# The last merge level's N: a copy on ScalarE in place of a masked product on VectorE

## The chip, the cores and the metric

The kernel runs on one core of a Trainium2 chip. The metric is the device time of one execution in microseconds (us); lower is better.

## What is computed

The reference is one transformer layer on an input of 4 sequences x 512 positions x 256: a gated delta-rule attention with 16 key heads and 32 value heads of width 128, a residual with layer norm, a mixture of 8 experts (top 2) plus a shared expert, and a second residual with layer norm. The attention is where nearly all of the time goes:

```python
def step(state, xs):
    q_t, k_t, v_t, g_t, b_t = xs
    state = state * jnp.exp(g_t)[..., None, None]
    kv = jnp.einsum('bhk,bhkv->bhv', k_t, state)
    delta = (v_t - kv) * b_t[..., None]
    state = state + jnp.einsum('bhk,bhv->bhkv', k_t, delta)
    out = jnp.einsum('bhk,bhkv->bhv', q_t, state)
    return (state, out)
```

The kernel computes this in chunks of 128 positions, and for each chunk and value head it needs the inverse of a 128x128 unit triangular matrix M that is made of keys, decays and betas.

## The kernel before, in words

**Bodies.** There are 64 bodies (`BODIES`), one for each pair of key head and sequence. A body has 4 chunks and 2 value heads, so 8 matrices M ("cells"), each 128x128. Six stages of work of up to four different bodies are interleaved: `ORDER` holds one list for each engine, written by hand, of entries (name, index, bodies ahead), and each engine walks through its own list once in each round. An engine carries out its list strictly in order. All waits are on semaphores that count finished operations.

**The inverse.** It is found by merging diagonal blocks: `X` holds the inverse of the blocks of size s in 16 bits, `XT` its transpose, and a level i joins blocks of size s = `LEVELS[i]` (2, 4, ..., 64) in pairs. A level has these steps:

- `join` on TensorE (L1024): 8 matmuls, one for each cell, of `mhiT` with the left column blocks of `X`, into PSUM bank `IB[1 - i % 2]`.
- `join` on VectorE (L1314): the product from PSUM times the mask `lev`, into `N[:, i]`. The mask keeps the diagonal and the block below it. For the last level (i = 5, s = 64) the left half of the columns is written, and the mask there is the identity in rows 0 to 63 and all ones in rows 64 to 127.
- `growx` on TensorE (L1034), a product of `XT` and `N`, and on ScalarE (L1215) the copy of it from PSUM into `X`.
- from level 2 on `growt` on TensorE (L1040) and on ScalarE (L1218), the same for `XT`.

`fill_n` (L838) sets all six parts of `N` to the identity once, at the start; later steps write only the left column blocks.

**After the last level.** `newton` (L1051, L1052) multiplies M with `X` for a correction, in two halves of 4 cells; half 0 waits for `X` of level 5 (`s_x`), half 1 for `XT` of level 5 (`s_xt`). Then VectorE's `res` (L1318) and TensorE's `finish` (L1059), VectorE's `tt` (L1324), and the chunk by chunk solution (`solve` L1075, `write` L1085, `read` L1063, `out` L1101 and L1102).

**Around the last level.** TensorE's list has, in this order: `solve` 3, `out` 2, `join` 5, `out` 3, `growx` 5, `growt` 5, `vtp` 0 to 2 (L992, transposes of v of a later body, which wait for ScalarE's `silu` 3), `newton` 0 and 1, `vtp` 3, `gate` 0 (L1001, which waits for ScalarE's `vals`). ScalarE's list has `u` 3 (L1223), `silu` 3 (L1183), `power` 0 (L1230: four squares, each with its accumulator read; it waits for VectorE's `og` 0), `growx` 5, `growt` 5, `vals` 0 (L1205), `power` 1, `vals` 1, `zs` 0 (L1211). VectorE's list has `conv` 10 and 11 (L1278), `og` 0 (L1351), `join` 5, `og` 1, `scan` 0 (L1284), `res` 0 and 1.

`silu` 3 and `vtp` belong to the body after the one whose levels are merged, `u`, `power` and `og` to the body of the round before.

The last round runs with the mixture of experts' first work in the free places (`drain`), and after it that part runs alone.

Of the kernel before, what the change touches and what calls it, by code (L numbers as in the profile page):

```python
# [9 lines left out]
ACT = mybir.ActivationFunctionType  # L10
# [11 lines left out]
LEVELS = [2, 4, 8, 16, 32, 64]  # L22
# [20 lines left out]
        ("proj", 6, 3), ("join", 3, 2), ("write", 2, 1), ("proj", 7, 3),  # L43
    ],
    "scalar": [
        ("growx", 3, 1), ("silu", 2, 2), ("growt", 3, 1), ("growx", 4, 1), ("growt", 4, 1), ("u", 3, 0),
        ("silu", 3, 2), ("power", 0, 0), ("growx", 5, 1), ("growt", 5, 1), ("vals", 0, 2), ("power", 1, 0),
        ("vals", 1, 2), ("zs", 0, 2), ("u", 0, 1), ("turn", 0, 0), ("tap", 0, 3), ("zs", 1, 2), ("tap", 1, 3),
        ("silu", 0, 3), ("turn", 1, 0), ("growx", 0, 2), ("u", 1, 1), ("squares", 0, 3), ("kraw", 0, 3),
# [1 line left out]
        ("growt", 2, 2), ("tap", 3, 3),  # L51
    ],
    "vector": [
        ("conv", 10, 2), ("conv", 11, 2), ("og", 0, 0), ("join", 5, 1), ("og", 1, 0), ("scan", 0, 2), ("res", 0, 1),
        ("res", 1, 1), ("tt", 0, 1), ("tt", 1, 1), ("scan", 1, 2), ("m", 0, 2), ("m", 1, 2), ("p", 0, 2), ("s", 0, 1),
        ("p", 1, 2), ("x0", 0, 2), ("conv", 0, 3), ("conv", 1, 3), ("rhs", 1, 1), ("conv", 2, 3), ("join", 0, 2),
        ("conv", 3, 3), ("acc", 0, 0), ("conv", 4, 3), ("turned", 0, 2), ("join", 1, 2), ("s", 1, 1), ("conv", 5, 3),
# [19 lines left out]
def build_kernel(nc, x_rows, x_cols, w_heads, w_ab, conv_w, dt_bias, a_log, gamma, w_out,  # L77
                 rms_w, router_w, gate_up, down, tri, levels16, neg_mask, ident16, iota8, exponents, out):
    ctx = ExitStack()
    with ctx:  # L80
# [3 lines left out]
        def sem(name):  # L84
            return ctx.enter_context(nc.semaphore(name))
# [3 lines left out]
        PB, IB, OB = bank[0:2], bank[2:4], bank[6:8]  # L89
# [22 lines left out]
        conv = sb("conv", [P, GROUPS, SEQ])  # L112
# [26 lines left out]
        N = sb("N", [P, len(LEVELS), CELLS, P], F16)  # L139
        res = mloT  # L140
# [4 lines left out]
        og = sb("og", [P, CELLS, P])  # L145
# [56 lines left out]
        s_np = sem("s_np")  # L202
        s_ident = sem("s_ident")
        s_n = sem("s_n")
        s_xgp = sem("s_xgp")
        s_x = sem("s_x")
        s_xtp = sem("s_xtp")
# [54 lines left out]
        def blocks(t, i, odd):  # L262
            s = LEVELS[i]
            return t.rearrange("p x (b two s) -> p x b two s", two=2, s=s)[:, :, :, odd]

        def packed(t, i):
            return t[:, :].rearrange("p (x b s) -> p x b s", x=CELLS, s=LEVELS[i])

        MATMUL_LEVELS = len(LEVELS) - TURNED

        def bank4(t):
            return t[:, :].rearrange("p (x n) -> p x n", x=4)
# [681 lines left out]
        def _(pe):  # L954
            gates_tensor(pe)

            def run(name, i, n):
# [67 lines left out]
                                       blocks(X[:, x:x + 1, :], i, 0), start=True, stop=True)  # L1025
                    mm.then_inc(s_np, 1)
                elif name == "growx":
                    pe.wait_ge(s_n, 6 * n + i + 1)
                    if 0 < i <= TURNED:
                        pe.wait_ge(s_xv, TURNED * n + i)  # L1030
                    if i > TURNED:
# [3 lines left out]
                                       start=True, stop=True)  # L1035
                    mm.then_inc(s_xgp, 1)
                elif name == "growt":
                    pe.wait_ge(s_n, 6 * n + i + 1)
                    for x in range(CELLS):
                        mm = pe.matmul(IB[1 - i % 2][:, x * 64:(x + 1) * 64], N[:, i, x, :], blocks(XT[:, x:x + 1, :], i, 1),  # L1040
                                       start=True, stop=True)
# [1 line left out]
                elif name == "newton":  # L1043
# [3 lines left out]
                    else:  # L1047
                        pe.wait_ge(s_xt, MATMUL_LEVELS * (n + 1))
                    for x in range(4):
# [110 lines left out]
        @block.scalar  # L1160
        def _(act):
            gates_scalar(act)
            act.wait_ge(s_const, CONSTS)

            def run(name, i, n):
                p, q, head = n % 2, n % 3, n // B
                if name == "tap":
                    g = COLS_OF[i]
                    act.wait_ge(s_proj, n * 4 + i + 1)
                    act.activation(conv[:, g, :], PB[i % 2][:, :], ACT.Copy,  # L1170
                                   scale=cw_all[:, head, g * TAPS + 3:g * TAPS + 4]).then_inc(s_tap, 1)
                elif name == "silu":
                    act.wait_ge(s_conv, 12 * n + 3 * i + 3)
                    if i == 0 and n > 2:
                        act.wait_ge(s_kq, 2 * (n - 2))
                        act.wait_ge(s_ksp, 3 * (n - 2))
                    if i == 1 and n > 1:
                        act.wait_ge(s_kq, 2 * (n - 1))
                        act.wait_ge(s_qe, n - 1)
                    if i == 2 and n > 0:  # L1180
                        act.wait_ge(s_vtp, 2 * n)
                    dst = (kT[:, q], qT[:, p], vT[:, 0], vT[:, 1])[i]
                    act.activation(dst, conv[:, COLS_OF[i], :], ACT.Silu).then_inc(s_silu, 1)  # L1183
                elif name == "squares":
                    act.wait_ge(s_ktp, n * 2 + i + 1)
                    if n > 0:
                        act.wait_ge(s_sq, 8 * (n - 1) + 4 * i + 4)
                    if n > 1:
                        act.wait_ge(s_ssk, n - 1)
                        act.wait_ge(s_epsq, n - 1)  # L1190
                    for c in range(CH):
                        act.activation(sqj[:, i, c, :], PB[i][:, c * P:(c + 1) * P], ACT.Square,  # L1192
                                       accum_out=ssum[:, p, i, c:c + 1]).then_inc(s_sq, 1)
                elif name == "kraw":
                    act.wait_ge(s_ktp, n * 2 + 1)
                    if n > 0:
                        act.wait_ge(s_keys, n)
                    act.activation(kraw[:, :, :], bank4(P0), ACT.Copy).then_inc(s_kraw, 1)  # L1198
                elif name == "vals":
                    act.wait_ge(s_vtp, n * 2 + i + 1)  # L1200
                    act.wait_ge(s_nk, n + 1)
                    if n > 1:
                        act.wait_ge(s_r, 6 * (n - 1))
                    for c in range(2):
                        act.activation(vals[:, p, 4 * i + 2 * c:4 * i + 2 * c + 2, :], bank4(PB[i])[:, 2 * c:2 * c + 2], ACT.Copy,  # L1205
                                       scale=nr[:, p, 0, 2 * i + c:2 * i + c + 1]).then_inc(s_vals, 1)
                elif name == "zs":
                    act.wait_ge(s_zp, n * 2 + i + 1)
                    if n > 1:
                        act.wait_ge(s_og, 2 * (n - 1))  # L1210
                    act.activation(zs[:, p, 2 * i:2 * i + 2, :], PB[i][:, :].rearrange("p (c n) -> p c n", c=2),  # L1211
                                   ACT.Silu).then_inc(s_zs, 1)
                elif name == "growx":
                    act.wait_ge(s_xgp, 6 * n + i + 1)
                    act.activation(blocks(X[:, :, :], i, 0), packed(IB[i % 2], i), ACT.Copy).then_inc(s_x, 1)  # L1215
                elif name == "growt":
                    act.wait_ge(s_xtp, MATMUL_LEVELS * n + i - TURNED + 1)
                    act.activation(blocks(XT[:, :, :], i, 1), packed(IB[1 - i % 2], i), ACT.Copy).then_inc(s_xt, 1)  # L1218
                elif name == "u":
                    act.wait_ge(s_up, n * 4 + i + 1)  # L1220
                    if n > 0:
                        act.wait_ge(s_pup, 2 * n)
                    act.activation(U[:, 2 * i:2 * i + 2, :], R1[:, 0:256].rearrange("p (v n) -> p v n", v=VH),  # L1223
                                   ACT.Copy, scale=1.0 if i else -1.0).then_inc(s_u, 1)
                elif name == "power":
                    act.wait_ge(s_og, n * 2 + i + 1)
                    if n > 0:
                        act.wait_ge(s_mse, n)
                    for x in range(4 * i, 4 * i + 4):
                        act.activation(og2[:, x, :], og[:, x, :], ACT.Square, scale=P ** -0.5,  # L1230
                                       accum_out=ms[:, 0, x:x + 1]).then_inc(s_ms, 1)
                elif name == "turn":
                    act.wait_ge(s_gtp, n * 2 + i + 1)
                    if n > 0:
                        act.wait_ge(s_opp, 2 * (n - 1) + i + 1)
                    act.activation(half(ogT, i), bank4(OB[i]), ACT.Copy).then_inc(s_gt, 1)  # L1236

            def drain(name, i, n):
                if (name, i, n) == ("growt", 3, BODIES - 1):
                    prepare_scalar(act, 3, 0)  # L1240
                elif (name, i, n) == ("power", 1, BODIES - 2):
                    prepare_scalar(act, 7, 0)
                elif (name, i, n) == ("u", 1, BODIES - 1):
                    gate_scalar(act, 0)
                elif (name, i, n) == ("u", 2, BODIES - 1):
                    gate_scalar(act, 1)
                    gate_scalar(act, 2)
                elif (name, i, n) == ("power", 1, BODIES - 1):
                    gate_scalar(act, 3)
                elif (name, i, n) == ("turn", 0, BODIES - 1):  # L1250
                    gate_scalar(act, 4)

            for name, i, n in rounds(ORDER["scalar"]):
                run(name, i, n)
                if n == 0 and (name, i) == ("tap", 0):
                    decays_scalar(act)
                if n == 0 and (name, i) == ("silu", 0):
                    rows_scalar(act)
                drain(name, i, n)
            moe_scalar(act)  # L1260
# [193 lines left out]
```

## Time and profile before

| | |
|---|---|
| median of 3 runs | 2317.08 us (2313.6 to 2317.55) |
| profiled execution, span from first to last instruction | 2315.6 us |
| profiled execution, own time outside the span | not listed; the median of the runs lies 1.5 us above the span |
| instructions | 53,894 |
| TensorE busy | 98% of the span |
| VectorE busy | 84% |
| ScalarE busy | 57% |
| GpSimd busy | 52% |
| round to round | 31.98 us |

Busy shares are means over the whole span. Within a round each engine's list has dense and thin stretches, so what the table says of ScalarE (57%) need not hold where the change is made. TensorE's matmuls are recorded from issue to end and overlap their neighbours; the times at which they start say more than their busy time.

### The profile page before, as it was taken

What the parts mean: (1) busy time and instruction counts of PE and PEld (TensorE: products, weight loads), DVE (VectorE), ACT (ScalarE), POOL (GpSimd) and SP (SyncE); (2) the same over time, 40 slices, a digit from 0 to 9 for tenths busy, and PEclk for the clock granted to TensorE, in tenths of its full rate; (3) what the DMA queues carried; (4) which work ended last, traced back from release to release, by engine and by line L of the source; (5) the groups of instructions that cost most, each with busy time, mean ns of one, the idle gap of its engine ahead of it and who ended that gap; (6) DMA issues with size and microseconds to landing.
All of it is one profiled execution on the core that took longest, in us unless ns stands there. A gap on an engine that the chain in (4) does not pass through costs nothing.

```text
span 2315.6 us, 53894 instructions
## 1 busy us (share of the span) xinstructions
PE 2275.0 (98%) x20046; PEld 1784.7 (77%) x20046; DVE 1953.3 (84%) x3427; ACT 1326.1 (57%) x4125; POOL 1204.2 (52%) x1199
## 2 busy tenths in 40 slices
PE   6899999999999999999999999999999999999998
PEld 3687888878888778888788887888877888776665
DVE  5788888888888888888888888888888888885665
ACT  4565666656666656666566665666666666653110
POOL 4456555555555556555655556565565655552100
PEclk8999999999999999999999999999999999999999
DMA  4011111111001110111110111101111010120000
GB/s 140 20 38 56 38 38 38 56 38 56 27 30 56 38 56 32 44 38 56 38 48 28 38 56 38 56 20 56 38 56 38 30 46 38 38 90 1 28 10 19
DMA packets 32115, 98.46 MB, mean 43 GB/s; under 512 B 4336, under 2 KB 9840, under 8 KB 31600
## 3 DMA queue, kind: packets, MB, share of 16 engines
q1 hardware_dynamic: 31856, 95.02, 11.8%
q8 instruction: 161, 2.64, 0.5%
q14 instruction: 98, 0.80, 0.1%
HBM read 92.39 MB, written 2.62 MB: 41 GB/s over the span
## 4 chain that ended last, share of the span: by engine, by line
PE 97%; DVE 2%; ACT 1%; issue 1%; DMA 0%; POOL 0%; POOLq 0%; DVEq 0%; SPq 0%; ACTq 0%
PE bank L974 19%; PE bank L1001 10%; PE bank L1120 10%; PE bank L1075 5%; PE bank L548 5%; PE bank L1102 5%; PE bank L1014 5%; PE bank L1101 4%; PE bank L1034 4%; PE bank L1085 4%; PE bank L1024 4%; PE bank L1063 4%; PE bank L984 3%; PE bank L992 3%; PE bank L1040 3%; PE bank L1110 3%
## 5 line engine op out<-in xcount | busy, mean ns | idle before, releaser
L1278 DVE SCALAR_TENSOR_TENSOR conv<-bank,cw_all,conv 128x511 f32<-128x511 f32 (+2 forms) x768 | 564.7, 742 | 45.2 <-ACT conv L1170 40.3
L974 PE MATMUL bank<-xT,w_kh 128*128 128x512 f32 x1024 | 531.0, 602 | 2.8 <-ACT kraw L1198 1.8
L1170 ACT ACTIVATE conv<-bank,cw_all 128x512 f32<-128x512 f32 x256 | 176.8, 691 | 245.4 <-PE bank L974 245.4
L1314 DVE TENSOR_TENSOR N<-bank,lev 128x512 f16<-128x512 f32 x384 | 258.9, 674 | 56.7 <-PE bank L1024 56.7
L1215 ACT ACTIVATE X<-bank 128x512 f16<-128x512 f32 x384 | 229.0, 596 | 100.6 <-PE bank L1034 100.6
L1120 PE MATMUL bank<-wo,ogT 128*128 128x256 f32 x1024 | 268.7, 385 | 0.0
L887 POOL TENSOR_TENSOR keys<-kraw,kfac 128x1024 f32<-128x1024 f32 x64 | 121.4, 1897 | 277.8 <-PE bank L1085 277.5
L1001 PE MATMUL bank<-w_kh,xT 128*128 128x256 f32 x1024 | 263.9, 391 | 0.1
L926 POOL TENSOR_TENSOR ms<-ms,epsq 128x8 f32<-128x8 f32 x64 | 12.8, 199 | 388.7 <-ACT og L1230 388.7
L1024 PEld LDWEIGHTS bank<-X,mhiT 128*128 128x128 f16 x3072 | 135.9, 98 | 101.0 <-issue 46.5
L1034 PEld LDWEIGHTS bank<-N,XT 128*128 128x128 f16 x3072 | 131.8, 98 | 106.3 <-DVE N L1314 52.8
L1223 ACT ACTIVATE U<-bank 128x256 f32<-128x256 f32 x256 | 100.9, 394 | 183.0 <-PE bank L1075 183.0
L1001 PEld LDWEIGHTS bank<-w_kh,xT 128*128 128x128 f32 x1024 | 180.7, 191 | 25.9 <-issue 1.0
L1120 PEld LDWEIGHTS bank<-wo,ogT 128*128 128x128 f32 x1024 | 180.2, 191 | 18.3 <-issue 1.0
L1102 PE MATMUL bank<-U,pT 128*128 128x128 f32 x1024 | 192.6, 280 | 0.0
L974 PEld LDWEIGHTS bank<-xT,w_kh 128*128 128x128 f32 x1024 | 161.2, 192 | 11.6 <-issue 3.3
L1192 ACT ACTIVATE sqj<-bank 128x128 f16<-128x128 f32 x512 | 134.4, 280 | 61.3 <-PE bank L984 61.2
L1308 DVE STREAM_TRANSPOSE XT<-X 128x1024 f16<-128x1024 f16 x128 | 158.7, 1240 | 9.0 <-ACT X L1215 0.7
L1034 PE MATMUL bank<-N,XT 128*128 128x64 f16 x3072 | 154.4, 193 | 9.5 <-DVE N L1314 9.5
L935 POOL TENSOR_TENSOR og<-og,ms 128x512 f32<-128x512 f32 x128 | 159.2, 1244 | 5.0
L1236 ACT ACTIVATE ogT<-bank 128x512 f32<-128x512 f32 x128 | 76.0, 593 | 149.6 <-PE bank L1110 149.6
L1101 PE MATMUL bank<-S,qE 128*128 128x128 f32 x768 | 158.7, 288 | 0.1
(181 smaller groups left out, 5651.2 us busy)
## 6 DMA issues: line engine op xcount, KB each, us to landing
egb<-rows SPq DMA_DIRECT2D x64, 512.0 KB, 4.9
ecb<-rows SPq DMA_DIRECT2D x64, 512.0 KB, 4.0
w_kh<-w_heads SPq DMA_DIRECT2D x16, 768.0 KB, 6.0
wo_raw<-w_out SPq DMA_DIRECT2D x16, 256.0 KB, 6.2
xT<-x_cols SPq DMA_DIRECT2D x4, 512.0 KB, 5.9
xT<-gate_up SPq DMA_DIRECT2D x1, 2048.0 KB, 7.7
ecb<-x_rows SPq DMA_DIRECT2D x3, 512.0 KB, 3.7
out<-og SPq DMA_DIRECT2D x3, 512.0 KB, 2.9
```

Source lines behind the costliest of these rows:

```text
L935: pool.tensor_tensor(half(og, i), half(og, i), ms[:, 2, 4 * i:4 * i + 4].unsqueeze(2).broadcast_to([P, 4, P]), ALU.mult).then_inc(s_on, 1)
L974: mm = pe.matmul(PB[j % 2][:, :], w[:, k, g * P:(g + 1) * P], xT[:, k, b * SEQ:(b + 1) * SEQ], start=(k == 0), stop=(k == KT - 1))
L1001: mm = pe.matmul(PB[h][:, 256 * c:256 * c + 256], xT[:, k, t * P:(t + 1) * P], w[:, k, 512:768], start=(k == 0), stop=(k == KT - 1))
L1024: mm = pe.matmul(IB[1 - i % 2][:, x * 64:(x + 1) * 64], mhiT[:, x, :], blocks(X[:, x:x + 1, :], i, 0), start=True, stop=True)
L1034: mm = pe.matmul(IB[i % 2][:, x * 64:(x + 1) * 64], XT[:, x, :], blocks(N[:, i, x:x + 1, :], i, 0), start=True, stop=True)
L1101: pe.matmul(dst, qE[:, p, x, :], S[:, c, v * P:(v + 1) * P], start=True, stop=False)
L1102: mm = pe.matmul(dst, pT[:, p, x, :], U[:, x, :], start=(c == 0), stop=True)
L1120: mm = pe.matmul(OB[h][:, 256 * c:256 * c + 256], ogT[:, 2 * i + v, :], wo[:, head % 2, v, :], start=(v == 0), stop=(v == VH - 1))
L1170: act.activation(conv[:, g, :], PB[i % 2][:, :], ACT.Copy, scale=cw_all[:, head, g * TAPS + 3:g * TAPS + 4]).then_inc(s_tap, 1)
L1215: act.activation(blocks(X[:, :, :], i, 0), packed(IB[i % 2], i), ACT.Copy).then_inc(s_x, 1)
L1278: dve.scalar_tensor_tensor(conv[:, g, m:], PB[j % 2][:, 0:SEQ - m], cw_all[:, head, g * TAPS + 3 - m:g * TAPS + 4 - m], conv[:, g, m:], op ...
L1314: dve.tensor_tensor(blocks(N[:, i], i, 0), packed(IB[1 - i % 2], i), blocks(lev[:, 1 + i:2 + i, :], i, 0).broadcast_to(shape), ALU.mult).t ...
```

## The change

At level 5 VectorE's multiplication by the mask is gone from its list. ScalarE gets a new entry `last`, between `u` 3 and `silu` 3, that copies partitions 64 to 127 of the product from PSUM to `N[:, 5]`. Partitions 0 to 63 are no longer written; they keep the identity of `fill_n`. TensorE's `growx` and `growt` of level 5 wait for the new semaphore `s_nlast`; those of the other levels wait for `s_n`, which now counts 5 for each body.

```diff
     "scalar": [
-        ("growx", 3, 1), ("silu", 2, 2), ("growt", 3, 1), ("growx", 4, 1), ("growt", 4, 1), ("u", 3, 0),
+        ("growx", 3, 1), ("silu", 2, 2), ("growt", 3, 1), ("growx", 4, 1), ("growt", 4, 1), ("u", 3, 0), ("last", 0, 1),
         ("silu", 3, 2), ("power", 0, 0), ("growx", 5, 1), ("growt", 5, 1), ("vals", 0, 2), ("power", 1, 0),
     "vector": [
-        ("conv", 10, 2), ("conv", 11, 2), ("og", 0, 0), ("join", 5, 1), ("og", 1, 0), ("scan", 0, 2), ("res", 0, 1),
+        ("conv", 10, 2), ("conv", 11, 2), ("og", 0, 0), ("og", 1, 0), ("scan", 0, 2), ("res", 0, 1),
@@ tensor, growx and growt
-                    pe.wait_ge(s_n, 6 * n + i + 1)
+                    if i < LAST_LEVEL:
+                        pe.wait_ge(s_n, LAST_LEVEL * n + i + 1)
+                    else:
+                        pe.wait_ge(s_nlast, n + 1)
@@ scalar
+                elif name == "last":
+                    act.wait_ge(s_np, 6 * n + 6)
+                    if n == 0:
+                        act.wait_ge(s_ident, len(LEVELS))
+                    act.activation(blocks(N[:, LAST_LEVEL], LAST_LEVEL, 0)[64:], packed(IB[0], LAST_LEVEL)[64:],
+                                   ACT.Copy).then_inc(s_nlast, 1)
```

## Rows read from the trace of the kernel before

**Rows 1.** The page: part 1 (TensorE), part 4 (the chain that ended last).

```profile
PE 2275.0 (98%) x20046; PEld 1784.7 (77%) x20046; DVE 1953.3 (84%) x3427; ACT 1326.1 (57%) x4125; POOL 1204.2 (52%) x1199
...
PE 97%; DVE 2%; ACT 1%; issue 1%; DMA 0%; POOL 0%; POOLq 0%; DVEq 0%; SPq 0%; ACTq 0%
```

**Rows 2.** Windows: stretch, its length, then busy time of each engine, PEclk.

```profile
1156.00:1163.00 7.00, 7.00 (x102) 6.53 (x99) 6.75 (x12) 6.27 (x19) 2.92 (x3) 1.00 0.01 4
```

**Rows 3.** Timeline of TensorE from join 5 on: start, length, instruction.

```profile
1160.03 0.40 PE L1024 MATMUL bank<-X,mhiT 128*128 128x64 f16 x8
1160.27 0.47 PE L1101 MATMUL bank<-S,qE 128*128 128x128 f32 x2
...
1160.79 0.39 PE L1101 MATMUL bank<-S,qE 128*128 128x128 f32 x2
1161.02 0.39 PE L1102 MATMUL bank<-U,pT 128*128 128x128 f32 x2
1161.29 0.41 PE L1034 MATMUL bank<-N,XT 128*128 128x64 f16 x8
...
1161.76 0.85 PE L992 MATMUL bank<-tri_sb,vT 128*128 128x128 f32 x6
1162.48 0.23 PE L1051 MATMUL bank<-X,mhiT 128*128 128x128 f16 x1
```

**Rows 4.** Timeline of VectorE, same stretch.

```profile
1160.55 0.68 DVE L1314 TENSOR_TENSOR N<-bank,lev 128x512 f16<-128x512 f32 x1
1161.44 0.69 DVE L1351 TENSOR_TENSOR og<-bank,zs 128x512 f32<-128x512 f32 x1 [0.21 <-PE bank L1102]
```

**Rows 5.** Timeline of ScalarE, same stretch.

```profile
1158.58 0.60 ACT L1215 ACTIVATE X<-bank 128x512 f16<-128x512 f32 x1 [0.61 <-PE bank L1034]
1159.07 0.59 ACT L1218 ACTIVATE XT<-bank 128x512 f16<-128x512 f32 x1
1159.55 0.39 ACT L1223 ACTIVATE U<-bank 128x256 f32<-128x256 f32 x1
1160.07 0.63 ACT L1183 ACTIVATE vT<-conv 128x512 f32<-128x512 f32 x1
1160.66 0.31 ACT L1230 ACTIVATE og<-og 128x128 f32<-128x128 f32 x1
...
1161.85 0.57 ACT L1215 ACTIVATE X<-bank 128x512 f16<-128x512 f32 x1
```

**Rows 6.** The same copy of level 5 in the first and last full round.

```profile
106.62 0.57 ACT L1215 ACTIVATE X<-bank 128x512 f16<-128x512 f32 x1
...
2057.21 0.57 ACT L1215 ACTIVATE X<-bank 128x512 f16<-128x512 f32 x1
```

**Rows 7.** Groups by line: ScalarE's copy of 64 partitions at the start.

```profile
L357 ACT ACTIVATE zs<-bank 64x512 f32<-64x512 f32 x2 | 1.2, 591 | 10.8 <-PE bank L389 10.8
```

**Rows 8.** ScalarE's timeline: a silu and the copy behind it.

```profile
1176.61 0.62 ACT L1183 ACTIVATE kT<-conv 128x512 f32<-128x512 f32 x1
1177.13 0.59 ACT L1236 ACTIVATE ogT<-bank 128x512 f32<-128x512 f32 x1
```

**Rows 9.** Timeline of VectorE: level 5 of body 0.

```profile
72.78 0.69 DVE L1314 TENSOR_TENSOR N<-bank,lev 128x512 f16<-128x512 f32 x1 [0.36 <-PE bank L1024]
```

**Rows 10.** Timelines of ScalarE and TensorE: level 5 of the last body.

```profile
2088.12 0.60 ACT L1215 ACTIVATE X<-bank 128x512 f16<-128x512 f32 x1 [0.32 <-PE bank L1034]
...
2086.24 0.40 PE L1024 MATMUL bank<-X,mhiT 128*128 128x64 f16 x8
```

**Rows 11.** Windows early and late (as rows 2), and TensorE's timeline at 2078.

```profile
82.00:90.00 8.00, 7.29 (x41) 4.66 (x39) 6.89 (x13) 2.32 (x5) 6.63 (x7) 1.00 0.01 2
...
2078.00:2080.00 2.00, 1.78 (x25) 1.73 (x26) 1.27 (x4) 0.61 (x2) 0.00 (x0) 0.66 0.48 172
2080.00:2082.00 2.00, 1.95 (x23) 1.73 (x21) 1.01 (x3) 0.86 (x2) 0.00 (x0) 0.50 0.03 11
...
2078.22 0.41 PE L1034 MATMUL bank<-N,XT 128*128 128x64 f16 x8 [3.28 <-DVE N L1314]
```

More of the change, by code:

```diff
@@ L204, in build_kernel @@
         s_n = sem("s_n")
+        s_nlast = sem("s_nlast")
         s_xgp = sem("s_xgp")
@@ L269, in build_kernel @@
         MATMUL_LEVELS = len(LEVELS) - TURNED
+        LAST_LEVEL = len(LEVELS) - 1
         def bank4(t):
@@ L1037, in run @@
                 elif name == "growt":
-                    pe.wait_ge(s_n, 6 * n + i + 1)
+                    if i < LAST_LEVEL:
+                        pe.wait_ge(s_n, LAST_LEVEL * n + i + 1)
+                    else:
+                        pe.wait_ge(s_nlast, n + 1)
                     for x in range(CELLS):
```

## The prediction

> **What bounds the kernel now.** I read the page first, then the chain of waits, then the timelines of three engines over the same seven microseconds of one round. The page says that TensorE is busy 98% of the span and that 97% of the chain that ended last is TensorE's [rows 1]. So what counts is whether TensorE is made to wait, and a microsecond taken off VectorE or ScalarE is worth nothing by itself. The shares of VectorE (84%) and ScalarE (57%) suggest that ScalarE has room and VectorE has not. That is the mean. In the stretch where the change is made ScalarE is busy 6.27 us of 7 and VectorE 6.75 of 7 [rows 2]: both are full there. The reader should therefore look at what each of them holds up at that place.
>
> VectorE first. TensorE's join 5 begins at 1160.03 and ends at 1160.43. VectorE's masked product begins at 1160.55, when og 0 makes room, and ends at 1161.23 [rows 3, 4]. In the meantime TensorE does out 3, and growx 5 begins at 1161.29. The last two pairs of out 3 begin at 1160.79 and 1161.02, 0.23 us apart [rows 3], so TensorE would have been ready at about 1161.24: the masked product costs TensorE 0.05 us in a round. After it VectorE idles 0.21 us until TensorE has ended out 3, and only then begins og 1 at 1161.44 [rows 4]. So VectorE's next work is released by TensorE, not by the end of the product, and taking the product away starts nothing sooner.
>
> ScalarE next. u 3 begins at 1159.55, silu 3 at 1160.07, power 0 at 1160.66, growx 5's copy at 1161.85 [rows 5], and with 6.27 us of work in 7 there is hardly a gap between them. Growx 5's matmuls end at 1161.29 + 0.41 = 1161.70 [rows 3], so the copy of X at 1161.85 waits for its place behind power 0, not for TensorE. It ends at 1161.85 + 0.57 = 1162.42 and newton 0 begins on TensorE at 1162.48 [rows 3, 5]. The six vtp matmuls before it began at 1161.76 and end at 1162.61 by the record, 0.85 us [rows 3]; but a matmul's record runs on while the next is issued (join 5's 0.40 beside the 0.24 after which its successor starts), and with some 0.16 us less for that TensorE is free at about 1162.45. The copy of X arrives just in time, with no slack at all. This is the place that decides: any delay of ScalarE's run from silu 3 to growx 5 goes into TensorE one for one.
>
> **The change part by part.** Removed: 64 masked products of 0.67 us on VectorE. By the above they are worth 0.05 us each on TensorE at growx 5, and VectorE's 0.6 us lies in front of a wait for TensorE, worth nothing.
>
> Added: one ScalarE copy of 64 partitions x 512 elements. The trace has this shape: the two copies of 64x512 from PSUM at the start take 591 ns, and the copies of 128x512 take 570 to 600 [rows 5, 7]. Half the partitions do not halve the time, and I take 0.59. What follows a copy starts 0.48 or 0.49 us after it (1158.58, 1159.07, 1159.55) [rows 5], because neighbours overlap; what follows a silu starts 0.52 after it (1176.61, 1177.13) [rows 8].
>
> Moved: everything on ScalarE behind it. The new copy waits for join 5, which ends at 1160.43, and ScalarE starts some 0.04 us after such an end, so it begins at 1160.47. Queued behind it are silu 3 (vtp 0 waits for it), power 0 (GpSimd's power and scaling of og wait for 0 and 1 together), growx 5 (newton 0), growt 5 (newton 1) and vals 0 (gate 0). Step by step:
>
> - silu 3: 1160.47 + 0.49 = 1160.96, where it was 1160.07. It ends at 1161.59, before vtp 0 would start (1161.76), so vtp is not held up.
> - power 0: 1160.96 + 0.52 = 1161.48, where it was 1160.66.
> - copy of X: power 0's eight instructions take 1161.85 - 1160.66 = 1.19 us, so 1162.67 to 1163.25, where it was 1161.85 to 1162.42: 0.82 to 0.83 later.
> - newton 0: from 1162.48 to about 1163.31, so TensorE idles about 0.83 us in front of it.
>
> The new N ends at 1160.47 + 0.59 = 1161.06, ahead of TensorE's 1161.24, so the 0.05 us at growx 5 is saved, but what stands behind it then waits for X all the same: it is part of the idle time at newton 0 and not a gain of its own. Growt 5's copy and vals 0 keep their distance from X, so newton 1 and gate 0 move by the same 0.83 and add nothing. Res, finish and tt on VectorE, and GpSimd's work on og, move with TensorE and ScalarE.
>
> Is it given back later? ScalarE has room after vals 1, TensorE has not: it issues without such gaps for the rest of the round, and the others wait for it. Nothing on TensorE is paced by something that this shift leaves where it was. So the round grows from 31.98 to 32.81 us.
>
> How many rounds: the same copy stands at 106.62 in the first round that has all this work and at 2057.21 in the last [rows 6]; (2057.21 - 106.62) / 31.98 = 61, so 62 rounds, each with the same 0.57 us and the same neighbours. Two bodies differ. Body 0 has no power 0 and no u 3 in front. VectorE's product runs from 72.78 to 73.47 there, straight after its wait for TensorE [rows 9]; ScalarE's copy is 0.1 us shorter, and this gains 0.1 us. In the last body join 5 ends at 2086.64 and the copy of X begins at 2088.12, released by TensorE [rows 10]. Now the new copy begins at 2086.68, power 0 at 2087.17, X at 2088.36: 0.24 us lost.
>
> Sum: 62 x 0.83 = 51.5; 51.5 - 0.1 + 0.2 = 51.6 us. The span 2315.6 becomes 2367.2. The median of the runs shown lies 1.5 us above the span, which gives 2368.7.
>
> Bounds of the unknown: the copy writes to partitions 64 to 127 only, of which no row exists. If it took its place at 0.40 us (the steps between ScalarE's copies are 0.48 and 0.49) the round would lose 0.74, in all 46 us: 2363. If nothing overlapped (0.59 for the copy, 0.63 for silu) it would lose 1.03, in all 64 us: 2381.
>
> **A rule against the trace.** The masked product has 0.68 us on VectorE and a copy 0.59 on ScalarE, and VectorE has the higher share of the two (84 against 57%) [rows 1, 4, 7]. The Trainium skill, page "Perfetto Trace Analysis", section "Optimizing Scalar/DVE Operations", says that where VectorE is saturated, handing some of its work to ScalarE may make sense. By that rule the change would be a gain; what it would be worth is the first rival below. The step it leaves out is that ScalarE is itself full at this place.
>
> **The rivals.**
>
> *Not slower.* ScalarE's delay is hidden, and what is left is the earlier growx 5: 0.05 us x 64 = 3 us, so 2314. For this newton 0 must find X ready at 1162.45, that is, ScalarE's run may slip by 0.03 us and no more, or TensorE must have 0.8 us of other work ready in front of newton 0. It has only the vtp matmuls, which it has already used. For it speaks VectorE's high share; against it all of rows 3 and 5. Chance 3%, nearly all of it within 0.2%.
>
> *Part of it comes back.* The longer round lets waits elsewhere shrink, for instance where TensorE waits for VectorE's N of level 4 behind two conv steps. If half of 0.83 is recovered: 62 x 0.42 = 26 us, 2343. Against it: those waits follow from TensorE's own matmuls of the level before and shift with it. Chance 7%.
>
> *Nothing overlaps on ScalarE,* or the copy waits longer for join 5: 2375 to 2381 as above. Chance 10%.
>
> *The clock falls.* After TensorE had idled 3.28 us up to 2078.22 the granted clock was 0.66 and 0.50 in the next two windows of 2 us, which is the lower of its levels (1.2 instead of 2.4 GHz) [rows 11]. Such a fall costs 2 x 0.34 + 2 x 0.50 = 1.7 us. If it came in each round: 62 x 1.7 = 105 us more, 2474. Against it: from 82 to 90 TensorE was busy 7.29 of 8 us and kept the clock at 1.00 [rows 11], and one idle time of 0.8 us in 32.8 is less. Chance 4%. The Trainium skill, "Perfetto Trace Analysis", section "Matmul Optimizations", says that TensorE scales its power with its use, so matmuls should come back to back; by that rule too an added idle time can cost more than itself, and the two windows agree with it for a long one.
>
> **How the numbers follow.** The forecast (2361 to 2375) has 76%, the four rivals 3, 7, 10 and 4%. The range must leave out no more than 2 in 10: from 2358 to 2380 it holds the forecast and nearly all of the case without overlap. A measurement of this kernel can tell about 0.2% (4.6 us) from no change. Slower by more than that has 96%, no change 3%, faster 1%.
>
> **What would show it.** In the changed profile: TensorE's waits get a line "matmul of newton (or its weight load) waits for ScalarE's X", some 0.8 us, in 62 rounds; the round is 32.8 us; silu 3 begins half a microsecond after the new copy; TensorE's busy share falls by some 2 points; and growx 5 follows out 3 without a gap. I am wrong if newton 0 still follows vtp 2 directly, if the round has shrunk somewhere else, or if windows in mid-run have a granted clock below 1.00.

## The result and the profile after

The changed kernel takes 2384.29 us (median of 4 runs, 2382.66 to 2385.7), the kernel before on the same chip 2317.32 us: a ratio of 1.0294 (95% interval 1.028 to 1.0309), 67.0 us slower. The forecast was 51.6 us slower, 2368.7, with a range up to 2380: the direction and the place were right, the size was short by 15 us, and the time lies outside the range.

These are the lines of the changed kernel's page that answer to [rows 1]:

```profile
PE 2286.1 (96%) x20046; PEld 1789.8 (75%) x20046; DVE 1921.7 (81%) x3363; ACT 1366.7 (57%) x4189; POOL 1203.8 (50%) x1199
...
PE 87%; ACT 7%; issue 4%; DVE 1%; POOL 1%; DMA 0%; POOLq 0%; DVEq 0%; SPq 0%
```

TensorE's share of the chain that ended last falls from 97 to 87%, and ScalarE has 7% of it where it had 1. TensorE's work is the same (20046 matmuls), VectorE has 64 instructions fewer and ScalarE 64 more. ScalarE's share of busy time is 57% as before; nothing on this line shows that it is now in the way.

The round's length comes from the copy of `kraw`, which stands once in a round. The lines are the row of this tile in a long stretch (count, shortest/median/longest ns, first and last start), first of the kernel before, then of the changed one:

```profile
L1198 ACT ACTIVATE kraw<-bank x40: 614/624/626, 604.2 to 1851.3; 128x512 f32<-128x512 f32 x40
```

```profile
L1206 ACT ACTIVATE kraw<-bank x39: 622/624/626, 621.5 to 1877.8; 128x512 f32<-128x512 f32 x39
```

(1851.3 - 604.2) / 39 = 31.98 us before, (1877.8 - 621.5) / 38 = 33.06 us after. The round has grown by 1.08 us, and 62 rounds of it are 67.0 us, the whole difference. The forecast had 32.81.

Now TensorE's timeline of one round of the changed kernel, from join 5 on (L1026), with out 3, growx 5 (L1039), growt 5 (L1048), vtp (L994) and newton 0 (L1059); it answers to [rows 3]:

```profile
1195.71 0.40 PE L1026 MATMUL bank<-X,mhiT 128*128 128x64 f16 x8
...
1196.69 0.39 PE L1110 MATMUL bank<-U,pT 128*128 128x128 f32 x2
1196.91 0.40 PE L1039 MATMUL bank<-N,XT 128*128 128x64 f16 x8
...
1197.44 0.87 PE L994 MATMUL bank<-tri_sb,vT 128*128 128x128 f32 x6
1199.23 0.23 PE L1059 MATMUL bank<-X,mhiT 128*128 128x128 f16 x1 [0.92 <-ACT X L1229]
```

Growx 5 begins 0.22 us after the last pair of out 3, where it was 0.27: the 0.05 us are there. Newton 0 begins 3.52 us after join 5 began, where it was 2.45, and the row names what it waited for: ScalarE's copy of X. In the kernel before, the table of waits of the whole run has this wait once, 0.6 us. In the changed kernel it has it 63 times (total us, times, longest us):

```profile
PEld bank L1059 <- ACT X L1229: 72.9, 63, 1.3
PE bank L1059 <- ACT X L1229: 58.1, 63, 1.2
```

And ScalarE's timeline of the same round, which answers to [rows 5]:

```profile
1195.22 0.39 ACT L1237 ACTIVATE U<-bank 128x256 f32<-128x256 f32 x1
1196.14 0.59 ACT L1225 ACTIVATE N<-bank 64x512 f16<-64x512 f32 x1 [0.53 <-PE bank L1026]
1196.76 0.63 ACT L1191 ACTIVATE vT<-conv 128x512 f32<-128x512 f32 x1
1197.29 0.29 ACT L1244 ACTIVATE og<-og 128x128 f32<-128x128 f32 x1
...
1198.37 0.19 ACT L1244 ACTIVATION_READ_ACCUMULATOR og<-og 128x1 f32 x1
1198.58 0.60 ACT L1229 ACTIVATE X<-bank 128x512 f16<-128x512 f32 x1
```

The reader should look at the steps from start to start. The new copy begins 0.43 us after join 5 (forecast 0.44) and lasts 0.59 (forecast 0.59). Silu 3 begins 0.62 after it, not 0.49: the copy ends at 1196.73 and silu starts only then. Silu to the first square is 0.53 (forecast 0.52). The copy of X begins 0.21 after the start of the last accumulator read, when that has ended (1198.56), where in the kernel before all such steps are about 0.09; and it lasts 0.60, where it was 0.57. So two steps have lost their overlap, 0.13 and 0.12 us, and the copy of X is 0.03 longer. In the other direction goes the first square, which took a step of 0.22 us before and takes 0.20 now. The sum, 0.26 us, is the difference between 0.83 and 1.08, to within the rounding of the rows. Why these two, when the other steps of ScalarE's list are as long as before, is what the experiments had to find out. An instruction that starts only when the one before it has ended is called held from here on.

### The profile page after: what moved, and what is told of

Its sections match the earlier page's. It is cut to its first block, busy times and chain, and to the rows that moved or that the text cites. A ratio compares the mean times of both kernels' runs of the same rounds, so it can differ in the third digit from the quotient of the medians.

```text
span 2384.0 us, 53894 instructions
## 1 busy us (share of the span) xinstructions
PE 2286.1 (96%) x20046; PEld 1789.8 (75%) x20046; DVE 1921.7 (81%) x3363; ACT 1366.7 (57%) x4189; POOL 1203.8 (50%) x1199
## 4 chain that ended last, share of the span: by engine, by line
PE 87%; ACT 7%; issue 4%; DVE 1%; POOL 1%; DMA 0%; POOLq 0%; DVEq 0%; SPq 0%
PE bank L976 18%; PE bank L1003 10%; PE bank L1128 9%; PE bank L1083 5%; PE bank L1016 5%; PE bank L550 5%; PE bank L1026 4%; PE bank L1093 4%; PE bank L1110 4%; PE bank L1071 3%; PE bank L1039 3%; ACT og L1244 3%; PE bank L1109 3%; PE bank L986 2%; PE bank L1118 2%
## 5 line engine op out<-in xcount | busy, mean ns | idle before, releaser
L1328 DVE TENSOR_TENSOR N<-bank,lev 128x512 f16<-128x512 f32 x320 | 215.4, 673 | 55.8 <-PE bank L1026 55.8
L1039 PEld LDWEIGHTS bank<-N,XT 128*128 128x128 f16 x3072 | 137.1, 98 | 102.7 <-DVE N L1328 51.9
L1026 PEld LDWEIGHTS bank<-X,mhiT 128*128 128x128 f16 x3072 | 135.8, 98 | 100.9 <-issue 46.5
L1039 PE MATMUL bank<-N,XT 128*128 128x64 f16 x3072 | 153.9, 193 | 9.4 <-DVE N L1328 8.7
```

The source lines that it names most:

```text
L1026: mm = pe.matmul(IB[1 - i % 2][:, x * 64:(x + 1) * 64], mhiT[:, x, :], blocks(X[:, x:x + 1, :], i, 0), start=True, stop=True)
L1039: mm = pe.matmul(IB[i % 2][:, x * 64:(x + 1) * 64], XT[:, x, :], blocks(N[:, i, x:x + 1, :], i, 0), start=True, stop=True)
L1328: dve.tensor_tensor(blocks(N[:, i], i, 0), packed(IB[1 - i % 2], i), blocks(lev[:, 1 + i:2 + i, :], i, 0).broadcast_to(shape), ALU.mult).t ...
```

## The experiments

### A copy over all 128 partitions

```diff
-                    act.activation(blocks(N[:, LAST_LEVEL], LAST_LEVEL, 0)[64:], packed(IB[0], LAST_LEVEL)[64:],
+                    act.activation(blocks(N[:, LAST_LEVEL], LAST_LEVEL, 0), packed(IB[0], LAST_LEVEL),
                                    ACT.Copy).then_inc(s_nlast, 1)
```

> The new ScalarE copy covers all 128 partitions instead of 64 to 127, everything else as in the changed kernel (rows 0 to 63 of N then hold the product itself instead of the identity). Theory A, that ScalarE does not overlap an instruction with the one before it where the starting partition differs from that of the last write to, or the last read from, the same memory: both steps close, silu 3 starts 0.49 us after the copy instead of 0.62 and the copy of X 0.09 after the last accumulator read instead of 0.21; the round loses 0.24 us, 62 rounds 15 us: 2369 us, where the forecast was. Theory B, that any copy put in this place waits like this (it follows a wait for TensorE, or ScalarE's queue runs dry): 2384 us, steps unchanged.

Measured: 2365.12 us against 2314.19 of the kernel before on that chip, a ratio of 1.0215 (1.0198 to 1.0232); the round is 32.78 us, from the row of `kraw`:

```profile
L1206 ACT ACTIVATE kraw<-bank x39: 621/623/625, 617.0 to 1862.6; 128x512 f32<-128x512 f32 x39
```

```profile
1186.84 0.60 ACT L1225 ACTIVATE N<-bank 128x512 f16<-128x512 f32 x1 [0.52 <-PE bank L1026]
1187.33 0.62 ACT L1191 ACTIVATE vT<-conv 128x512 f32<-128x512 f32 x1
...
1188.92 0.19 ACT L1244 ACTIVATION_READ_ACCUMULATOR og<-og 128x1 f32 x1
1189.02 0.58 ACT L1229 ACTIVATE X<-bank 128x512 f16<-128x512 f32 x1
```

Both steps close: 0.49 and 0.10. With twice the partitions the copy lasts 0.60 us where it lasted 0.59, and the round is 0.28 us shorter. This kernel leaves the mask out (rows 0 to 63 of `N` hold the product where the identity belongs), so it measures the hold and is no replacement for the changed kernel. Theory B falls. The forecast's own arithmetic (32.81, and 51 us slower) describes this kernel, not the one that was asked for: the difference here is 50.9 us.

### 64 partitions, but the lower ones

```diff
-... LAST_LEVEL, 0)[64:], packed(IB[0], LAST_LEVEL)[64:],
+... LAST_LEVEL, 0)[:64], packed(IB[0], LAST_LEVEL)[:64],
```

> The copy covers partitions 0 to 63 in place of 64 to 127 (so rows 64 to 127 of N are never updated: this part of the merge is left out). Theory A, the starting partition counts: steps 0.49 and 0.09, about 2369 us, as with 128 partitions. Rival, the number of partitions counts (64 against 128 in the neighbours): steps 0.62 and 0.21, 2384 us.

Measured: 2366.76 us in one run, a round of 32.76 us, steps of 0.49 to 0.50 and 0.09 to 0.10. This kernel leaves out the rows of `N` that the merge needs. The number of partitions plays no part; where they start does.

### Reads and writes apart

```diff
-... LAST_LEVEL, 0)[64:], packed(IB[0], LAST_LEVEL)[64:],
+... LAST_LEVEL, 0)[64:], packed(IB[0], LAST_LEVEL)[:64],
```

> The copy reads partitions 0 to 63 of the bank and writes partitions 64 to 127 of N (N then holds other rows: the last merge is wrong in value). Theory A with reads and writes apart: the write sets the memory of silu 3's hold, so silu 3 still starts 0.62 us after the copy; the read from PSUM started at partition 0, so the copy of X starts 0.09 us after the accumulator read. 0.12 x 62 = 7 us less than the changed kernel, 2377 us. Rival, one cause for both steps: both stay (2384) or both go (2369).

```diff
-... LAST_LEVEL, 0)[64:], packed(IB[0], LAST_LEVEL)[64:],
+... LAST_LEVEL, 0)[:64], packed(IB[0], LAST_LEVEL)[64:],
```

> The mirror image: the copy reads partitions 64 to 127 of the bank and writes partitions 0 to 63 of N (N holds other rows: the last merge is wrong in value). Theory A: silu 3 starts 0.49 us after the copy (its write starts where the last one did, and it reads SBUF), while the copy of X, the next to read PSUM, still starts 0.21 us after the accumulator read. About 2377 us. Rival, one cause for both steps: 2384 or 2369.

Measured: 2372.52 and 2378.62 us, one run each, where about 2377 was expected of both, and rounds of 32.91 and 32.93 us. Both kernels put other rows into `N` than the merge needs. The rounds differ by 0.02 us and the single times by 6. Most of the 6 us lies before the rounds: in the first 80 us TensorE's mean granted clock was 0.94 in the first of the two and 0.85 in the second, and the same copy of `kraw` stands at 614.9 and at 619.7 us. So the rounds and the steps are the better evidence. ScalarE's timeline where the copy reads partition 0 on and writes partition 64 on:

```profile
1187.05 0.59 ACT L1225 ACTIVATE N<-bank 64x512 f16<-64x512 f32 x1 [0.53 <-PE bank L1026]
1187.66 0.63 ACT L1191 ACTIVATE vT<-conv 128x512 f32<-128x512 f32 x1
...
1189.28 0.18 ACT L1244 ACTIVATION_READ_ACCUMULATOR og<-og 128x1 f32 x1
1189.37 0.57 ACT L1229 ACTIVATE X<-bank 128x512 f16<-128x512 f32 x1
```

And where it reads partition 64 on and writes partition 0 on:

```profile
1192.10 0.59 ACT L1225 ACTIVATE N<-bank 64x512 f16<-64x512 f32 x1 [0.53 <-PE bank L1026]
1192.60 0.62 ACT L1191 ACTIVATE vT<-conv 128x512 f32<-128x512 f32 x1
...
1194.19 0.19 ACT L1244 ACTIVATION_READ_ACCUMULATOR og<-og 128x1 f32 x1
1194.40 0.60 ACT L1229 ACTIVATE X<-bank 128x512 f16<-128x512 f32 x1
```

Reads and writes hold different instructions. A write that starts at partition 64 holds the next instruction that writes SBUF from partition 0 (silu 3: 0.61 against 0.50). A read of PSUM that starts at 64 holds the next instruction that reads PSUM from partition 0, and that is the copy of X, with nine instructions in between (0.21 against 0.09); silu and the squares in between read SBUF and are not held. The two prices, 0.13 and 0.15 us a round against 32.78, add up to the 0.28 of the changed kernel.

The Trainium skill states this for VectorE, on the page "VectorE: DVE Perf Modes", section "Two Vector instructions with no wait between them": an instruction is held until all earlier ones have finished where its input or output starts in another quarter of the partitions than the last read from, or the last write to, the same memory. The section speaks of Vector instructions only. On ScalarE the changed kernel and these four variants of its copy agree with it, with 0.12 to 0.13 us for each hold. They tried starts at 0 and 64 alone, and of the two orders only the instruction at 0 behind one at 64: the new copy itself waits for TensorE, so a hold in front of it would not show.

### The copy twice

A second copy of the same 64 partitions into a scratch area (the squares' unread output `sqj`), directly in front of the first (the semaphore `s_extra` and the squares' wait for it are not shown):

```diff
+                    act.wait_ge(s_sq, 8 * min(n + 1, BODIES - 1) + 8)
+                    act.activation(sqj[64:, 0].rearrange("p c (y s) -> p (c y) s", s=64),
+                                   packed(IB[0], LAST_LEVEL)[64:, :, 0], ACT.Copy).then_inc(s_extra, 1)
                     act.activation(blocks(N[:, LAST_LEVEL], LAST_LEVEL, 0)[64:], packed(IB[0], LAST_LEVEL)[64:],
```

> A second, useless copy of the same 64 partitions of the bank (into a scratch area) directly in front of the new one on ScalarE. Theory, ScalarE's delay reaches TensorE one for one through the copy of X: the second copy adds one step of 0.49 us (same starting partitions, so it overlaps) to each of 62 rounds, 30 us: 2415 us. Rival, the delay is partly absorbed further on or newton is held by something else: clearly less than 30 us. Rival, it also makes growx 5 late (N would end 0.3 us after TensorE is ready): no more than the same 30 us, since newton waits behind it anyway.

Measured: 2415.89 us in one run, the round 33.55 us, 0.49 longer than the changed kernel's. ScalarE's timeline:

```profile
1211.59 0.59 ACT L1229 ACTIVATE sqj<-bank 64x512 f16<-64x512 f32 x1 [0.53 <-PE bank L1027]
1212.09 0.58 ACT L1231 ACTIVATE N<-bank 64x512 f16<-64x512 f32 x1
1212.69 0.63 ACT L1192 ACTIVATE vT<-conv 128x512 f32<-128x512 f32 x1
```

Two copies that both start at partition 64 overlap (0.50), the silu behind them does not (0.60). The whole 0.49 us reaches the end of every round: nothing absorbs a delay of ScalarE at this place.

### No product at all

The changed kernel without the new copy; level 5's `N` stays the identity, so this kernel leaves the product out. The second change stands in `growx` and again in `growt`:

```diff
-("u", 3, 0), ("last", 0, 1),
+("u", 3, 0),
-                        pe.wait_ge(s_nlast, n + 1)
+                        pe.wait_ge(s_ident, len(LEVELS))
```

> The changed kernel without the new copy: level 5's N is never computed and stays the identity, and growx 5 waits for nothing on that account (this part of the computation is left out). It gives the most that taking the product off VectorE can be worth. Theory: newton 0 is held by the copy of X behind power 0 as before, so at most 0.05 us a round: 2313 to 2317 us. Rival, VectorE's 0.6 us is worth something by itself: 62 x 0.6 = 37 us, 2280 us.

Measured: 2318.06 us, a ratio of 1.0005 (0.9994 to 1.0015), and a round of 31.97 us. TensorE's timeline:

```profile
1157.70 0.39 PE L1110 MATMUL bank<-U,pT 128*128 128x128 f32 x2
1157.92 0.40 PE L1039 MATMUL bank<-N,XT 128*128 128x64 f16 x8
...
1159.16 0.23 PE L1059 MATMUL bank<-X,mhiT 128*128 128x128 f16 x1
```

```profile
1158.53 0.57 ACT L1229 ACTIVATE X<-bank 128x512 f16<-128x512 f32 x1
```

Growx 5 now starts 0.22 us after out 3's last pair and newton 0 still starts 0.06 us after the copy of X ends at 1159.10. This settles what the change could have gained: taking the masked product off VectorE is worth nothing that can be measured, even when nothing takes its place. VectorE's 0.6 us went into a longer wait for TensorE in front of og 1, 0.81 where it was 0.21 [rows 4]:

```profile
1158.12 0.69 DVE L1365 TENSOR_TENSOR og<-bank,zs 128x512 f32<-128x512 f32 x1 [0.81 <-PE bank L1110]
```

### The squares behind the urgent copies

```diff
-("silu", 3, 2), ("power", 0, 0), ("growx", 5, 1), ("growt", 5, 1), ("vals", 0, 2), ("power", 1, 0),
-("vals", 1, 2),
+("silu", 3, 2), ("growx", 5, 1), ("growt", 5, 1), ("vals", 0, 2), ("power", 0, 0), ("vals", 1, 2),
+("power", 1, 0),
```

In the changed kernel:

> The changed kernel with ScalarE's list reordered: the squares of power 0 and 1 go behind the copies that TensorE waits for (new copy, silu 3, growx 5, growt 5, vals 0, power 0, vals 1, power 1). Theory, the loss is only the place of the copy of X behind power 0: X is ready 0.05 us after growx 5's matmuls plus 0.6, newton 0 starts directly behind vtp 2 again, and the time comes back to that of the kernel before, 2314 to 2320 us. Rival, the squares are now what is late: GpSimd's power and scaling start 1.5 us later, so its mask steps and VectorE's start of the next inverse too, and some of it reaches TensorE: 2330 to 2360 us.

The same list in the kernel before:

> The kernel before with the same reordering of ScalarE's list alone (VectorE still does the masked product). Theory: the copy of X there was 0.15 us later than TensorE's growx 5 allowed, but newton 0 had only 0.03 us of it to gain: 2314 to 2317 us, no difference that can be measured. If the later squares cost something, it shows here without the change: above 2322 us.

And in the kernel with the copy over 128 partitions:

> The changed kernel with both mends: the copy over all 128 partitions (no holds on ScalarE) and the squares behind the copies that TensorE waits for. Theory, with the squares late it is GpSimd's chain from the squares to the next inverse's start that sets the round (it did so in the kernel before with the same list too, 32.28 us a round): the missing holds change nothing, 32.28 us a round, 2334 us. Rival, the holds in front of silu 3 still count: 0.13 us a round less, 2326 us.

Measured: 2336.77 us (ratio 1.0089, 1.0072 to 1.0106), 2334.34 us (1.0077, 1.006 to 1.0094) and 2331.1 us (one run); rounds of 32.29, 32.28 and 32.22 us. The new order takes back 0.77 of the 1.08 us, and stops there, with the new copy or without it: something else now sets the round, and it costs the kernel before 0.30 us that it did not pay. My expectation for the kernel before (no difference) was wrong, and for the changed kernel it was the rival (2330 to 2360 us) that came true and not the theory. The page of the kernel before with this list no longer has a chain of TensorE's, 97% [rows 1], but this one:

```profile
PE 37%; issue 30%; POOL 19%; DVE 12%; POOLq 1%; ACT 1%; DMA 0%; DVEq 0%; SPq 0%
```

And these are rows of its table of waits in a stretch of 1280 us:

```profile
POOL ms L926 <- ACT og L1230: 299.0, 39, 7.7
PEld bank L1034 <- DVE N L1314: 60.5, 160, 0.6
DVE X L1305 <- POOL XT L917: 54.4, 40, 1.4
```

GpSimd waits up to 7.7 us for the squares, where it was 5.9, and then has its power, its scaling of og and its masks to do in this order, with TensorE's next inverse behind them: VectorE's start of that inverse waits 1.4 us in each round for GpSimd's `XT`, for which it waited twice in the whole run of the kernel before, and TensorE's growx waits for N four times a round instead of twice. That this chain sets the round is read from the trace; no run made GpSimd's part shorter. The last kernel, without holds, was 0.07 us a round shorter, between the two expectations: the holds cost 0.28 us a round in the changed kernel's order and 0.07 in this one.

### The last level left out

The copy of N, the masked product and what they feed belong to level 5, and the kernel without a product had shown that the round does not depend on it. So the level was taken out as a whole, and the correction that follows (newton, res, finish, tt) stands for the last merge alone. On paper this is enough: if X holds the exact inverses A and D of the two diagonal blocks and C is the block of M below them, one step X + X(I - MX) puts -DCA below them, which is the block of the exact inverse. What is given up is that this block, too, is first computed in 16 bits and then corrected. Not shown are the counts of the waits, and a wait of newton 0 for `XT`:

```diff
-LEVELS = [2, 4, 8, 16, 32, 64]
+LEVELS = [2, 4, 8, 16, 32]
@@ tensor
-("out", 2, 0), ("join", 5, 1), ("out", 3, 0), ("growx", 5, 1), ("growt", 5, 1),
+("out", 2, 0), ("out", 3, 0),
@@ scalar
-("power", 0, 0), ("growx", 5, 1), ("growt", 5, 1), ("vals", 0, 2)
+("power", 0, 0), ("vals", 0, 2)
@@ vector
-("og", 0, 0), ("join", 5, 1), ("og", 1, 0)
+("og", 0, 0), ("og", 1, 0)
```

> The kernel before without level 5 of the merge at all: join, growx and growt of block size 64 are left out on TensorE (24 small matmuls a round), VectorE (the masked product) and ScalarE (two copies); the newton, res, finish and tt steps that follow are one correction of X by the residual, and they alone stand for the last merge. Theory, TensorE's own list sets the round and newton then follows vtp 2 directly: 3 groups x 0.235 us and the 0.05 and 0.03 us of waiting around them are gone, 0.78 us a round, 62 rounds 48 us: about 2269 us. Rival, something else is as tight: the squares and vals on ScalarE or GpSimd's chain from the squares to the next inverse keep the round near 31.7: 2300 us.

Measured: 2275.2 us against 2314.67, a ratio of 0.9834 (0.9816 to 0.9852); the round is 31.35 us, 0.63 shorter and not 0.78. The chain of this kernel, in order of time, shows what came between:

```profile
1104.43 0.04 DVE og L1352
1104.47 0.57 issue
1105.04 0.98 DVE decb L1285
1106.02 0.16 issue
1106.17 1.27 DVE mloT L1319 x2
```

VectorE had waited 0.56 us for out 3 with og 1, then did scan 0 (`decb`), and only then res (`mloT`), for which the second half of TensorE's finish now waited:

```profile
1106.93 0.39 PE L1060 MATMUL bank<-XT,mloT 128*128 128x128 f16 x4
1107.49 0.40 PE L1060 MATMUL bank<-XT,mloT 128*128 128x128 f16 x4 [0.17 <-DVE mloT L1319]
```

So scan 0 was moved into the wait:

```diff
-("og", 0, 0), ("og", 1, 0), ("scan", 0, 2), ("res", 0, 1),
+("og", 0, 0), ("scan", 0, 2), ("og", 1, 0), ("res", 0, 1),
```

> The kernel without level 5, and VectorE's scan 0 moved in front of og 1, into the 0.56 us in which VectorE waits for TensorE's out 3. In the run without level 5 the chain went through og 1, scan 0 and res, and finish's second half waited 0.17 us for res. Theory, that wait is all that is left there: 0.16 us a round less, 62 rounds 10 us, about 2265 us. Rival, og 1 now ends 0.6 us later, and power 1 with it, and GpSimd's chain from the squares takes the gain back: 2275 us.

Measured: 2254.34 us against 2316.62, a ratio of 0.9736 (0.9719 to 0.9754), the best version here. The round is 31.00 us; it gained 0.35 and not 0.16. The 0.17 us of the row counts from the end of the first half's record, which runs on while the next matmul could start. From start to start the second half came 0.56 us after the first. In the new kernel the eight matmuls of finish stand in one row and gate 1 follows 0.45 us after its start (1097.12), so a half takes about 0.22 and the wait had cost 0.34:

```profile
1096.67 0.61 PE L1060 MATMUL bank<-XT,mloT 128*128 128x128 f16 x8
```

Against the kernel before, the round is 0.98 us shorter and not 0.78: from out 2's last pair to newton 0 it is 1.83 us where it was 2.67, and from newton 0 to gate 1 it is 2.49 where it was 2.63, which the expectation did not have. The chain is TensorE's again:

```profile
PE 97%; DVE 2%; ACT 1%; issue 0%; DMA 0%; POOL 0%; POOLq 0%; DVEq 0%; SPq 0%
```

## Why the prediction was wrong in size

**What bounds the kernel, and that the masked product is worth nothing: right.** Growx 5 gained its 0.05 us and newton took it again; without any product the round is 31.97 against 31.98 us.

**The place: right.** Newton 0 waits for the copy of X in every round, silu 3 and vtp hold up nobody, newton 1 and gate 0 keep their distance (in the changed kernel gate 0 begins 1.22 us after newton 0, before 1.21). The copy twice shows that a delay of ScalarE there passes to the end one for one, and nothing is given back later: the second rival falls. The clock was 1.00 in the stretch from 600 to 1880 us of the changed kernel, so the fourth falls as well: the idle time of 0.92 us a round did not lower it.

**The size: the step that failed is "What follows a copy starts 0.48 or 0.49 us after it".** It was read from rows whose instructions all start at partition 0. The new copy starts at 64, and that makes ScalarE finish it before silu 3 starts: 0.62. I had written that no row of such a copy existed and put the unknown into the length of the copy, which is 0.59 as in the row of 64 partitions at the start; it was in the step behind it. The sign that silu 3 would begin half a microsecond after the new copy did not come true for this reason.

**The same cause broke a step that I had carried over unchanged, "power 0's eight instructions take 1.19 us".** To the start of the copy of X it is 1.29 (0.12 for the hold, less the 0.02 of the first square), because the first read of PSUM from partition 0 after a read from 64 waits for all before it. I priced the case in which nothing overlaps at 1.03 us and 10%; it has one hold at the copy and lets silu lose its overlap too, which it kept (0.53), and it has none at the copy of X. The measured 1.08 is above it, so the upper bound was too low as well. With the copy on 128 partitions the sum of the prediction comes out: 32.78 against 32.81 us.

**The number of rounds: right.** 62 x 1.08 = 67.0 us is the whole difference of the medians.

**The advice of the Trainium skill** that where VectorE is saturated, handing work to ScalarE may make sense ("Perfetto Trace Analysis", section "Optimizing Scalar/DVE Operations") did not pay here: the kernel became 2.9% slower. Both engines were full at this place, and only ScalarE's work stood in front of something that TensorE needed at once.

What stays open: the holds were measured with starts at 0 and 64 only and in one order only, 0 behind 64, and why a held copy of X lasts 0.03 us longer is not known. It is the length that a copy of X has in the kernel before where it starts behind idle time (0.60 at 1158.58 [rows 5], 0.60 at 2088.12 [rows 10]).

## What to carry to other kernels

Before moving an operation between engines, look at what stands behind it in the new engine's list in that stretch, and at who waits for the first of those results; a mean share of busy time says nothing about it, and here an engine busy 57% of the time had 6.27 us of work in the 7 that mattered [rows 2]. When an operation touches only some partitions, let it start at the partition where its neighbours' reads and writes start: a copy of all 128 partitions cost the round 0.28 us less than one of 64 that starts at partition 64. (That copy left the mask out, so it shows the price and not a way to save it.) And before making a step cheaper, ask whether it is needed: leaving the whole level out gained 2.6%, with scan 0 moved into the wait that this opened.

## What the runs showed of the hardware

On ScalarE an instruction that writes SBUF from partition 0 on after a write that started at 64, or that reads PSUM from partition 0 on after a read that started at 64, did not overlap the one before it: 0.12 to 0.13 us each, and for reads the effect reached over nine instructions that read SBUF to the next that read PSUM. A copy of 64x512 and one of 128x512 from PSUM last the same, 0.59 and 0.60 us. The granted clock stayed at 1.00 in mid-run with one idle time of 0.92 us in a round of 33 us.
